# Third layer of a four-layer kernel: attention scores on row tiles, values on column tiles, the division behind them, expert tokens stationary

## What is computed

```python
# attention: 16 heads of width 16; one key head and one value head for all
q = rope(hidden @ Wq.T)          # the angle depends on the head alone here
k = rope(hidden @ Wk.T); v = hidden @ Wv.T
scores = einsum('bhqd,bokd->bhqk', q, k) * 16 ** -0.5, causal
attn = einsum('bhqk,bokd->bhqd', softmax(scores), v) @ Wo.T
# experts: 16, the best 4 of each token, at most 128 tokens each, width 176
mid  = silu(xg @ w_gate[e]) * (xg @ w_up[e])
y[tokens of e] += (mid @ w_down[e]) * weight
y   += shared expert of width 352
```

## Time and profile before

| | us |
|---|---|
| runs, median (lowest, highest) | 1128.98 (1126.83, 1131.62) |
| the profiled execution | 1134.37 |
| its span, first to last instruction | 1132.6 |
| third layer's route stage, about | 507.9 to 585.4 |
| third layer's attention and expert stage | 585.5 to 772.4 |

### The profile page before, as it was taken

The page is one execution under the profiler, slowest core; times in us unless marked ns, Lnnn a source line. Parts: engine busy times, 40 slices in busy tenths (PEclk is TensorE's granted clock), DMA queues, the critical chain, the costliest instruction groups (busy, mean ns, idle before and its releaser), DMA issues. The chain is left out here.

```text
span 1132.6 us, 14814 instructions
## 1 busy us (share of the span) xinstructions
PE 1010.6 (89%) x4900; PEld 666.6 (59%) x4900; DVE 756.2 (67%) x1218; ACT 498.8 (44%) x1135; POOL 379.1 (33%) x284
## 2 busy tenths in 40 slices
PE   5799867965999999859979989996899989999997
PEld 4355554624566566545558868884566658555554
DVE  3689965325999999757628868827566640765762
ACT  3542324266888788334124434423566641111112
POOL 0379910005888788510011221210355540000000
PEclk9899988885999999878889999997999999999999
DMA  4112104003000000022022332381000000101001
GB/s 118 39 60 85 50 16 156 1 7 107 19 25 24 19 26 4 1 59 65 1 87 61 87 86 67 83 233 57 1 2 2 1 1 12 45 30 53 28 0 38
DMA packets 53917, 52.55 MB, mean 46 GB/s; under 512 B 10088, under 2 KB 48840, under 8 KB 53856
## 3 DMA queue, kind: packets, MB, share of 16 engines
q1 hardware_dynamic: 50256, 47.05, 13.8%
q0 software_dynamic: 3072, 4.20, 2.2%
q10 hardware_dynamic: 528, 0.52, 0.1%
HBM read 44.19 MB, written 5.47 MB: 44 GB/s over the span
## 5 line engine op out<-in xcount | busy, mean ns | idle before, releaser
L1017 POOL TENSOR_TENSOR seen<-state,c_row 128x512 f32<-128x512 f32 x128 | 160.5, 1275 | 39.9 <-PE banks L1155 27.7
L1037 DVE TENSOR_TENSOR_SCAN state<-decay,banks 128x512 f32<-128x512 f32 x128 | 155.5, 1217 | 21.0 <-issue 7.3
L2300 PE MATMUL banks<-xnT,weight 128*128 128x512 f32 x256 | 115.0, 593 | 1.0 <-PEq L2027 1.0
L976 ACT ACTIVATE weighed_x<-dx_tok,b_tok 128x512 f32<-128x512 f32 x128 | 90.1, 709 | 25.3 <-PE banks L1141 25.0
L2034 POOL TENSOR_TENSOR prob<-prob,inverse 128x512 f32<-128x512 f32 x64 | 65.2, 1039 | 107.5 <-DVE inverse L2119 107.5
L1141 PEld LDWEIGHTS banks<-ident,weighed_x 128*128 128x128 f32 x512 | 59.5, 142 | 63.9 <-ACT weighed_x L976 40.5
L986 ACT ACTIVATE decay<-delta_pairs,A 128x510 f32<-128x510 f32 x128 | 90.5, 707 | 6.3 <-DVE state L1037 6.2
L1141 PE MATMUL banks<-ident,weighed_x 128*128 128x128 f32 x512 | 81.0, 282 | 6.9 <-ACT weighed_x L976 6.0
L2341 DVE TENSOR_TENSOR inter<-gelu,banks 128x512 f32<-128x512 f32 x32 | 22.0, 688 | 96.7 <-ACT gelu L2332 96.1
L2332 ACT ACTIVATE gelu<-banks 128x512 f32<-128x512 f32 x32 | 19.1, 597 | 138.2 <-PE banks L2300 138.2
L2300 PEld LDWEIGHTS banks<-xnT,weight 128*128 128x128 f32 x256 | 48.7, 190 | 49.2 <-issue 47.7
(11 more groups left out here) (363 smaller groups left out, 2046.8 us busy)
## 6 DMA issues: line engine op xcount, KB each, us to landing
prob_row<-probs_dram SPq DMA_DIRECT2D x8, 512.0 KB, 4.2
c_row<-c_dram SPq DMA_DIRECT2D x32, 128.0 KB, 2.9
slot_gate_w<-in_L_ffn_w_gate SPq DMA_DIRECT2D x16, 176.0 KB
slot_up_w<-in_L_ffn_w_up SPq DMA_DIRECT2D x16, 176.0 KB
slot_down_w<-in_L_ffn_w_down SPq DMA_DIRECT2D x16, 176.0 KB
gate_up_w<-in_L_ffn_gate_up_w SPq DMA_DIRECT2D x8, 256.0 KB, 4.3
delta_pairs<-conv_in SPq DMA_DIRECT2D x8, 256.0 KB, 3.4
w_WqT<-in_L_attn_W_q SPq DMA_DIRECT2D x1, 2048.0 KB, 10.0
```

Of the source, the lines that this page charges most:

```text
L976: nc.scalar.activation(weighed[:, v % 2, tile, :, j, :], dx_tok[:, 4 * p + tile, :].rearrange("p (g e) -> p g e", g=groups), ACT.Identity, ...
L1017: nc.gpsimd.tensor_tensor(seen[:, u % ring, :], state[:, u % ring, :], c_row[:, v % 4, :], ALU.mult).then_inc(seen_ready, 1)
L1037: nc.vector.tensor_tensor_scan(state[:, u % ring, :], decay[:, u % ring, :, :].rearrange("p b t -> p (b t)"), banks[:, 4 + u % 2, :], 0.0, ...
L2300: last = nc.tensor.matmul(banks[:, 4 + 2 * half + j, :], weight[:, s, j, k, tile * P:(tile + 1) * P], xnT[:, k, cols[half]], start=(k == 0 ...
```

## The change

In `route_stage` the rotation is folded into the weights: POOL computes Wq * cos + Wq_swap * sin (with the scale of the scores in both), in three operations that wait for the late loads, and q is one product, emptied by ACT alone. Keys are kept in two masked copies instead of eight. v gets a column of ones and 15 of zeros beside its 16.

In the other stage there are still 48 units of 512 columns. Four units that differ in their 32 rows of q (two heads each of every group of eight) make a group, with a score bank for each. The scores of two units are issued together, on two tiles of 32 rows (L1736). The probabilities keep their sums out of ACT. After the transposes, v is stationary (32 columns) and the probabilities stream, 512 or 256 columns at a time, the four units of a group on four tiles of 32 columns in one bank (L1762, L1765). Row 16 of each tile is the sum. ACT copies the bank (`o_raw`, 8 times in all); SP moves the four rows of sums to 128 partitions, DVE inverts them, SP stores them and loads them back spread over 32 partitions each; POOL divides into `oT`, which is already feature by token, at 32 rows for each head. The product with Wo (spaced likewise, so four blocks instead of two) is done per sequence inside the loop (L1776). Experts come every two and a half units. Their tokens are stationary and both wide weights stream in one product of 352 columns per half (L1793); the middle is then turned by PE and copied by ACT. All transposes and expert results share two banks in one sequence of turns: turn n waits until turn n - 2 is emptied.

```diff
-                    wide = {"k": ("Wk", "Wk"), "q": ("Wq", "Wq_swap"), "s": ("sw_gate", "sw_up")}[kind]
+                    wide = {"k": ("Wk", "Wk"), "q": ("Wq",), "s": ("sw_gate", "sw_up")}[kind]
...
+    first_wide = [(5 * e) // 2 - 1 for e in range(EXPERTS2)]
...
+                def begin_turn(kind, i):
+                    n = turn_of[kind, i]
+                    if n >= 2:
+                        turn_emptied(pe, *turns[n - 2])
+                    return turn_bank(kind, i)
...
+                        for r in (first_row, first_row + 1):
+                            tile = slice(r * rows, (r + 1) * rows)
+                            last = nc.tensor.matmul(banks[:, r, 2 * j * n_keys:2 * (j + 1) * n_keys],
+                                                    q[tile, kd, first:first + P], keys[tile, :, b * SEQ:b * SEQ + n_keys],
...
+                    for kt in range(1 if kind == 0 else 2):
+                        for r in range(group):
+                            u = g * group + r
+                            out = banks[r * rows:(r + 1) * rows, 6, :]
+                            if kind == 0:
+                                last = nc.tensor.matmul(out, v[:, 2 * b, :], probT[:, u % 8, :], start=True, stop=True,
...
+                for step in steps:
+                    if 0 <= step < units:
+                        turn(step)
+                        if step % 2 and step + 3 < units:
+                            score(step // 2 + 2)
+                    if step % group == 1 and 0 <= step // group - 1 < groups:
+                        weigh(step // group - 1)
+                    for n in sums_at(step - 8):
+                        if n % 2:
+                            mix(n // 2)
...
+                def invert(n):
+                    dve.wait_ge(sums_moved, DMA * (n + 1))
...
+                for step in steps:
+                    for n in sums_at(step):
+                        move_sums(n)
+                    for n in sums_at(step - 2):
+                        store_inverses(n)
+                    for n in sums_at(step - 4):
+                        spread_inverses(n)
...
+                    for e in experts_at(step, 4):
...
+                        if e == EXPERTS2 - 1:
+                            for dst, src in next_loads:
+                                sp.dma_start(dst, src).then_inc(next_loaded, DMA)
+                            sp.wait_ge(scattered, DMA * EXPERTS2)
+                            sp.dma_start(gated[:, :, :], y_dram[0:N, :].rearrange("(n p) d -> p n d", p=P)).then_inc(y_loaded, DMA)
```

More of the change, by code:

```diff
@@ new lines, in heads_of, with experts_at, sums_at @@
+    def heads_of(u):
+        return 4 if part_of(u)[1] == 0 else 2
+    def experts_at(step, lag):
+        return [e for e in range(EXPERTS2) if first_wide[e] + lag == step]
+    def sums_at(step):
+        g = step // group - 1
+        return [2 * (g // 3) + (g % 3) // 2] if step % group == 1 and 0 <= g < groups and g % 3 != 1 else []
+    steps = range(-1, units + 10)
+    turns = []
+    for step in steps:
+        if 0 <= step < units:
+            turns.append(("prob", step))
+        turns += [("mix", n // 2) for n in sums_at(step - 8) if n % 2]
+        turns += [("x", e) for e in experts_at(step, 0)]
+        turns += [("mid", e) for e in experts_at(step, 3)]
+        turns += [("low", e) for e in experts_at(step, 4)]
@@ L1527, in attention_and_expert_stage, with emptied_count @@
+    turn_of = {name: n for n, name in enumerate(turns)}
+    on_vector = [kind in ("prob", "low") for kind, _ in turns]
+    def emptied_count(n):
+        return sum(on_vector[i] == on_vector[n] for i in range(n + 1))
     with ExitStack() as ctx:
         m = Core(nc, ctx)
-        q_now = m.sbuf("q_now", [P, 2, 2, SEQ])
-        top = m.sbuf("score_top", [P, 4, group])
-        shift = m.sbuf("score_shift", [P, 4, group])
-        total = m.sbuf("prob_total", [P, 4, group])
-        inverse = m.sbuf("prob_inverse", [P, 4, group])
@@ new lines, in _ @@
+                score(0)
+                score(1)
+                for step in steps:
+                    if 0 <= step < units:
+                        turn(step)
[6 more added lines that the diff above has]
+                            mix(n // 2)
+                    for e in experts_at(step, 0):
+                        turn_tokens(e)
+                    for e in experts_at(step, 1):
+                        widen(e)
+                    for e in experts_at(step, 3):
+                        turn_mid(e)
+                    for e in experts_at(step, 4):
+                        lower(e)
@@ new lines, in _ @@
+                for u in range(group):
+                    top(u)
+                for step in steps:
+                    if 0 <= step < units:
+                        keep_turned(step)
+                        if step and step + 3 < units:
+                            top(step + 3)
+                    for n in sums_at(step - 2):
+                        invert(n)
+                    if step == units + 4:
+                        for b in range(NT // 2 - 1):
+                            finish(b)
+                    for e in experts_at(step, 2):
+                        middle(e)
+                    for e in experts_at(step, 4):
+                        weigh_result(e)
@@ new lines, in _ @@
+                exps(0)
+                for step in steps:
+                    if 0 <= step and step + 1 < units:
+                        exps(step + 1)
+                    if step == units:
+                        act.wait_ge(y_loaded, DMA)
+                        for b in range(NT // 2):
+                            pair = slice(2 * b, 2 * b + 2)
+                            nc.scalar.activation(gated[:, pair, :], gated[:, pair, :], ACT.Silu).then_inc(gate_ready, 1)
+                    for n in sums_at(step):
+                        keep_sums(n)
+                    for n in sums_at(step - 8):
+                        if n % 2:
+                            keep_mixed(n // 2)
+                    for e in experts_at(step, 0):
+                        copy_tokens(e)
+                    for e in experts_at(step, 1):
+                        gate(e)
+                    for e in experts_at(step, 3):
+                        copy_mid(e)
```

538 lines of the change are left out of this document (259 added, 279 removed).

## The result

The changed kernel takes 1124.58 us (median of 20 runs, 1120.4 to 1132.3) against 1131.39 for the kernel before, timed beside it (20 runs, 1126.8 to 1136.7): a ratio of 0.995, interval 0.993 to 0.997. It is 6.8 us faster, where the forecast was 2.7 slower. 1124.6 lies inside the range of 1116 to 1148, but the sign is the other one.

What follows compares the result with a forecast made beforehand. PE was taken to bound the loop, DVE close behind at 83%. About 18 us won before N and 20.8 given back behind it make +2.7: 1128.98 + 2.7 = 1131.7, said as 1132; 8-in-10 range 1116 to 1148.

Steps and rivals of the forecast that it cites:

- a group of values at 1.7 us: Loop, PE: 16 records of 256 columns on four column tiles take 1.7 us, between ends of 1.06 and 3.4.
- entries of 0.3 us: Loop, PE: 0.3 us added for entering each pair of scores and each group of values.
- 0.4 us a step for uneven work: Loop: uneven work keeps PE and DVE from reaching their own sums and adds about 0.4 us a step.
- Route stage: Third layer's norms and route: dropping Wq_swap's product gains 2.7 us, with 1.5 and 3.4 as ends.
- Start of the loop: From the loop stage's start at 582.8 to the end of DVE's first transpose copy at 591.5: 8.7 us.
- Step: Loop, one unit: 3.05 us against 3.15 before, over 39 steps 119 us, plus 6.8 for two products with Wo.
- the case with four tiles at once: Loop: values on four column tiles all run together, 1.06 us a group, step 2.9, 6 us less in all.
- The end: Behind SP's first next-layer issue (N): engines stand 16 us for the seventh sums until N + 24; stage ends N + 57.5.
- the end is not held by the bulk: Stage's end: seventh sums don't wait for weights and y, N + 14 not N + 24, 10 us less; within faster's 0.28.
- slower: Loop: PE and DVE take full turns, costlier tile entry or column tiles sharing one stream; 1135 to 1161, chance 0.35.
- Won and given back: Changed stage: about 18 us won before SP's first next-layer issue (N), 20.8 given back behind it.
- faster rival: End not held by bulk, 10 us less (1122); with four tiles at once 6 less (1116); 1112 to 1125, chance 0.28.

Runs made afterwards that it cites:

- values_one: Changed kernel with all four matmul chains of a group of values on one column tile, one after the other: 1148.0 us, 1.016 to the kernel before.
- route_only: Kernel before with only q's weights turned by cos and sin on POOL and Wq_swap's product left out: 1127.1 us, ratio 0.997.
- values_two: Changed kernel with the four chains of a group of values on two column tiles in turn, not four: 1131.4 us, 1.000 to the kernel before.
- no_mask: Changed kernel without DVE's 48 additions of the causal mask: 1121.9 us, 0.991 to the kernel before.

## Why the prediction was wrong

**The step that failed is the size of one term: a group of values at 1.7 us.** It measured 1.07. The difference makes (1.7 - 1.07)/4 = 0.16 us a step, 6.1 us over 39 steps, of the 7.0 by which the loop was overstated. The forecast had the right value as its lower end and chose the one "nearest to the rows with two". That was a poor way to choose: in the earlier trace rows two tiles overlapped fully, 8 records in the time of 4, and no row spoke for the overlap ending at two. A row that shows one chain's own stream for as many tiles as were used asks to be carried on, not to be split with the serial end. The runs on two tiles and on one show the term alone: they give the loop 6.7 us for 0.84 us a group and 25.7 for 2.55, so 0.63 us a group are 5.0 to 6.3, and with two tiles the kernel is no faster than before (1.000). With this term right the sum would have been +2.7 - 6.1 = -3.4, and the sign with it. The stage measured -6.6 (267.2 against 273.8); of the other 3.2 us 1.4 lie ahead of the loop, 0.9 in it and 0.9 behind it.

That the rest of the loop seems right hides errors that cancel. The entries of 0.3 us for the group and for each pair were not seen (1.00 and 1.06 from start to start). Against them, four blocks of transposes took about 0.55 us instead of 0.47, and an expert 2.7 instead of 2.5. All of it makes 9.6 us of PE per four steps instead of 10.6, 10 us over the loop, and the forecast, which had PE's clock at full speed there, missed the loop at full clock by 126.1 - 115.2 = 10.9. The 4.0 us that the clock took hid a part of that. The 0.4 us a step for uneven work came out about right. The Trainium skill, TensorEngine Tiling (Array Packing), says "up to 4x" under Theoretical Speedup. The trace agrees: 3.62 / 1.07 = 3.4 from one tile to four.

The other points, in the order of the forecast:

- **Route stage**: 3.5 us won, 2.7 forecast. PE's clock behind the pause was 0.70 over the q products (8 records in 5.15 us); POOL's three operations took 1.26 to 1.31, not 1.04; nobody waited for them, but DVE was slower beside them (below). The run of this part alone gives 3.2.
- **Start of the loop**: 8.1 us to the first copy's end, 8.7 forecast.
- **Step**: (119.1 - 6.8)/39 = 2.88 us, 3.05 forecast, the 2.9 of the case with four tiles at once; at full clock 2.78. That neither engine reaches its sum (2.65 and 2.5) held: PE stands 12 us and DVE 32 in the loop, 13 of these for transposes and 12 for the experts' last product.
- **The end**: 56.6 us behind N, 57.5 forecast. DVE's invert came at N + 22.0 after 14.75 us of waiting, forecast N + 24 and 16. PE and ACT stood with it, and PE came out of it cold twice, as written. The rival "the end is not held by the bulk" (N + 14) was wrong: the loads moved out of the way gave 10.6 us, and that was the 10 us that it had priced.
- **The rival "slower"** asked for column tiles that share one stream. It is out with the 1.07 us. Values one after the other were priced at 0.43 us a step, 17 us, above 1.7 us for a group; above the 1.07 that four tiles take the same sum gives 23, and values_one took 23.4 us more than the changed kernel.
- **Won and given back**: N comes 26.5 us sooner than before, counted from the third layer's first issue (210.7 and 237.2), forecast 18; behind it 19.9 are given back, forecast 20.8. What the forecast did not show is whose cost this is: without the bulk the kernel before wins 4 to 6 us, the changed one 10.7 and then 9 more.

The chances were drawn with 0.28 on faster, and the faster rival's two gains (10 and 6 us) were held together at the low end. One came and the other did not, which is -3.3; the case of four tiles alone had no chance of its own, and it is the nearest to the result of -6.8.

## What to carry to other kernels

Where a tile position is in no row but its neighbour is, take what the neighbour does as it stands and scale it, and give the whole of its failure a chance apart; don't average the mechanism away. When a loop is made shorter, look at what is queued where it ends. Large loads for the next stage, issued in one go in the queue that also carries the small ones of this stage's end, cost 4 to 6 us while other work still held the stage's end, and 10.7 once it did not; spreading them over the loop was worth more here than the whole change, and cost the loop nothing. Then look for the next one in line: a wait for a late transfer also holds what stands behind it on its own engine, as ACT's gating held its copy of the sums.

## What the hardware showed that was not expected

- Four column tiles of 32 run at once in full with f32 records of 256 columns: 16 records in 1.07 us, 1.91 on two tiles, 3.62 on one. Two row tiles of 32 rows: 1.13 us against 1.98 on one.
- DVE slowed beside POOL. The first of its comparisons of 128x2048 took 2.29 us in the kernel before and 3.31 here, where POOL's last operation on q's weights overlaps it by 1.15 us (513.24 to 514.39) and so costs it 1.02. The next one, behind POOL's last, took 2.28. The twelve profiles with POOL's turning part the same way: in the eight where it overlaps, the comparison took 3.30 or 3.31 us, and in the four where POOL had ended before (route_only, values_two, values_one, no_mask) 2.29:

```profile
513.13 1.26 POOL L1326 TENSOR_TENSOR w_Wq<-w_Wq,w_Wq_swap 128x512 f32<-128x512 f32 x1
513.24 3.31 DVE L179 TENSOR_TENSOR above<-score 128x2048 f32<-128x2048 f32 x1
...
516.47 2.28 DVE L180 TENSOR_TENSOR equal<-score 128x2048 f32<-128x2048 f32 x1
```

- The same code in layers 1 and 2 ended at 491.8 to 498.6 us in fourteen profiles, the route stage had PE's lower clock for some 10 us more in one of them, and the same loop was 0.8 to 4.2 us short of full clock in six. A profile's end time says little on an edit of a few us; the piece between two marks around it says more, and most with the granted clock of that piece beside it.
